# Two-layer steps of a conditioned layer pair: ScalarE's gelu halves before yt and x_hi, GpSimd's second low half before its power, VectorE's x_lo after the second statistics

## The reference, cut to what matters

```
kind 0 or 1:  out = gelu(x @ w1 + b1) @ w2 + b2            (two layers)
kind 2:       out = gelu(gelu(x @ w1 + b1) @ w2 + b2) @ w3 + b3   (three layers)
x1  = layernorm(x + out) * gamma + beta
h   = gelu(x1 @ down_W.T + down_b)
h   = h @ expert_W[domain].T + expert_b[domain] + domain_emb[domain]
out = layernorm(h @ up_W.T + up_b + x1) * ln_gamma + ln_beta
```

## Time and profile before

| | |
|---|---|
| median of 3 runs | 278.79 us (278.51 to 279.04) |
| profiled execution, own time | 277.94 us |
| its span | 276.1 us |
| TensorE matmuls | 252.9 us busy, 92% of the span |
| VectorE | 203.0 us, 74% |
| ScalarE | 191.2 us, 69% |
| GpSimd | 174.7 us, 63% |
| granted TensorE clock, mean | 0.985 |

### The profile page before, as it was taken

The page is one execution under the profiler, slowest core; times in us unless marked ns, Lnnn a source line. Parts: engine busy times, 40 slices in busy tenths (PEclk is TensorE's granted clock), DMA queues, the critical chain, the costliest instruction groups (busy, mean ns, idle before and its releaser), DMA issues.

```text
span 276.1 us, 8026 instructions
## 1 busy us (share of the span) xinstructions
PE 252.9 (92%) x2114; PEld 219.2 (79%) x2115; DVE 203.0 (74%) x715; ACT 191.2 (69%) x450; POOL 174.7 (63%) x190
## 2 busy tenths in 40 slices
PE   7998999999999988999999999999999999999850
PEld 7798889989989977878887777788888888778630
DVE  6779453294495485878888877888888888878871
ACT  3587579668768765867777777777777777777730
POOL 3134565455876876867777677677776777677480
PEclk9999999999999999999999999999999999999995
DMA  6373011101212202232323222333232323222224
GB/s 181 101 251 70 6 36 42 23 22 40 61 39 58 67 28 57 67 85 80 91 76 95 76 76 79 83 85 82 80 85 77 94 76 95 76 77 71 54 66 92
DMA packets 41640, 20.71 MB, mean 75 GB/s; under 512 B 37431, under 2 KB 39181, under 8 KB 41614
## 3 DMA queue, kind: packets, MB, share of 16 engines
q1 hardware_dynamic: 37785, 12.23, 18.5%
q0 software_dynamic: 2592, 7.08, 7.3%
q10 hardware_dynamic: 1236, 1.06, 1.5%
HBM read 11.69 MB, written 8.65 MB: 74 GB/s over the span
## 4 chain that ended last, share of the span: by engine, by line
PE 58%; ACT 13%; issue 11%; DVE 8%; POOL 5%; DMA 2%; DVEq 1%; ACTq 1%; SPq 1%; POOLq 0%
PE ps_h L1082 18%; PE ps_z L1150 12%; PE ps_t L1172 9%; PE ps_z L1155 6%; ACT yt L931 5%; ACT x_hi L883 4%; ACT h_hi L897 3%; POOL h_lo L481 2%; PE ps_z L1117 2%; PE ps_u L1202 2%; PE ps_t L1253 2%; POOL rs L488 1%; PE ps_t L1256 1%; PE ps_t L1254 1%; DMA out<-o 1%
## 5 line engine op out<-in xcount | busy, mean ns | idle before, releaser
L481 POOL TENSOR_TENSOR h_lo<-h,h_hi 128x256 fp32r<-128x256 f32 (+1 forms) x75 | 70.6, 942 | 45.3 <-ACT h L897 42.1
L488 POOL TENSOR_TENSOR rs<-ve,minus_half 128x4 f32<-128x4 f32 (+1 forms) x38 | 41.0, 1079 | 32.2 <-DVE ve L699 32.0
L904 ACT ACTIVATE zn<-ps_z,nm,rs 128x256 f32<-128x256 f32 x66 | 33.7, 562 | 31.4 <-DVE nm L703 30.9
L687 DVE BATCH_NORM_STATS2 st<-ps_z 128x6 f32<-128x256 f32 x66 | 24.9, 418 | 31.5 <-PE ps_z L1155 31.5
L897 ACT ACTIVATE h_hi<-ps_h,per_feature_sb 128x256 fp32r<-128x256 f32 x84 | 38.9, 496 | 12.3 <-PE ps_h L1082 8.2
L931 ACT ACTIVATE yt<-ps_t,per_feature_sb 128x256 f32<-128x256 f32 x66 | 34.1, 574 | 17.5 <-PE ps_t L1172 17.4
L1150 PE MATMUL ps_z<-last_hi,h_hi 128*128 (+1 forms) x132 | 35.8, 305 | 6.7 <-ACT h_hi L897 6.7
L897 ACT ACTIVATE h<-ps_h,per_feature_sb 128x256 f32<-128x256 f32 x84 | 38.8, 498 | 0.0
L661 DVE TENSOR_TENSOR x_lo<-x,x_hi 128x512 fp32r<-128x512 f32 x33 | 23.5, 712 | 19.8 <-ACT x_hi L883 19.8
L1202 PE MATMUL ps_u<-tables,stack 65*64 x132 | 35.6, 392 | 0.3 <-ACT stack L915 0.3
L1202 PE MATMUL ps_u<-second_table,stack 65*64 65x256 f32 x132 | 35.5, 392 | 0.0
(11 more groups left out here) (150 smaller groups left out, 658.3 us busy)
## 6 DMA issues: line engine op xcount, KB each, us to landing
x<-in_x_feat SPq DMA_DIRECT2D x130, 64.0 KB
out<-o SPq DMA_DIRECT2D x20, 64.0 KB, 2.0
out<-o,out_rows_now POOLq DMA_INDIRECT x54
last_sb<-in_last_w SPq DMA_DIRECT2D x1, 768.0 KB, 5.0
w_sr_sb<-in_w_sr SPq DMA_DIRECT2D x1, 512.0 KB, 4.0
w_sr_sb<-in_w_sr ACTq DMA_DIRECT2D x1, 512.0 KB, 5.0
w_two_sb<-in_w_two SPq DMA_DIRECT2D x1, 512.0 KB, 5.6
per_unit_sb<-in_per_unit SPq DMA_DIRECT2D x1, 268.1 KB
```

Of the source, the lines that this page charges most:

```text
L481: pool.tensor_tensor(dst, full, high.bitcast(F32), ALU.subtract).then_inc(ready, 1)
L488: pool.tensor_tensor(RS[p][:, norms, :], VE[p][:, norms, :], half_of_two[:, norms, :], ALU.pow).then_inc(rstd, 1)
L904: ins = act.activation(ZN[:, t, :], ZP[p][:, t, :], ACT.Identity, bias=NM[p][:, t:t + 1], scale=RS[p][:, 0, t:t + 1])
```

## The change

Three lists are reordered; no instruction is added or dropped.

ScalarE: in two-layer steps the second gelu half comes straight after the first, ahead of `yt` and `x_hi`. In the step in which the last three-layer slot is finished, `yt` stays first and both gelu halves follow. GpSimd: in the same steps the low half of the second gelu comes ahead of the power. VectorE: in every step up to the last but two, the statistics of `ps_u` come ahead of `x_lo`, and their moments behind it.

```
@@ gpsimd, step of a two-layer slot
                 with pool.Else():
                     for slot in on_slot(g, -1, where):
                         low(h2l[:, 0, :], h2[:, 0, :], h2h[:, 0, :], h0_full, h0_lo, g + 1)
-                    powers(g, i, p, where)
                     for slot in on_slot(g, -1, where):
                         low(h2l[:, 1, :], h2[:, 1, :], h2h[:, 1, :], h1_full, h1_lo, g + 1)
+                    powers(g, i, p, where)
@@ vector
                 variances(p, BOTH)
+                for slot in on_slot(g, 2, where):
+                    second_stats(slot, p)
                 for slot in on_slot(g, -2, where):
                     input_low(slot, p)
                 for slot in on_slot(g, 2, where):
+                    second_moments(slot, p, q)
                     if where == LAST2:
-                        last_variances(slot, p, q)
-                    else:
-                        second_stats(slot, p)
-                        second_moments(slot, p, q)
+                        dve.wait_ge(stat[1], 2 * TT * slot + 2 * TT)
+                        variances(q, SECOND)
@@ scalar
                         with act.If(g < b_sr):
...
                             for k in kind:
                                 first_of_two(k, True)
+                                second_of_two(k)
                         with act.Else():
                             for k in kind:
                                 first_of_two(k, False)
+                                second_of_two(k)
                             for slot in on_slot(g, 1, where):
                                 residual_norm(slot, q, where)
                     next_input(g, i, p, where)
-                    for k in kind:
-                        second_of_two(k)
```

More of the change, by code:

```diff
@@ L991, in _ @@
                         first_of_two(kind[0], False)
+                        second_of_two(kind[0])
                     else:
```

## The result

The changed kernel takes 283.27 us (median of 4 runs, 283.00 to 283.64) where the kernel before takes 278.92 in the same job (4 runs, 278.51 to 279.66). The ratio is 1.0151, with a 95% interval from 1.0128 to 1.0174: 4.35 us slower, where I had predicted 5.8 us faster. The time lies inside the range, the direction was wrong. The profiled execution took 283.44 us.

The account below looks back on a forecast made before the run. ScalarE's order was taken to set the 6.37 us two-layer step. 277.94 - 5.1 - 1.0 + 0.2 = 272.0 us profiled, 273.0 forecast for the median, range 267.5 to 284.0.

Parts of the forecast that it names:

- The step that failed: GpSimd, low half ahead of the power: cost 0 in the steady step, stores out about 1.2 us earlier.
- The mechanism of the late signals: TensorE's signals in dense steps: cause unknown; second gelu half assumed to start 0.2 us beyond 208.33.
- Second gelu ahead of `yt`: ScalarE, two-layer steps: removes the last layer's wait for `h_hi`, gaining 0.23 us a step, 5.1 us over 22 steps.
- GpSimd, the single places: Step after the three-layer ones and last two-layer step: waits for the low half go, net 0.6 and 0.4 us.
- VectorE, 0 and +0.2 us: `x_lo` behind the statistics of `ps_u`: 0 in the steady step, 0.2 us lost in all in three-layer steps.
- The slow rival: ScalarE: second gelu waits for its late signal, `yt` behind it; +0.37 us a step, 286.1 us on the median; chance 0.23.
- The fast rival: TensorE waits for nothing, its own stream bounds: steps of 5.9 us, 267.4 us on the median; chance 0.22.
- The density reading: Full internal trace-record queues can hold an engine back, so a denser step would keep its late signals; no run showed it.

Follow-up runs that it names:

- holding job: Any of the three follow-up jobs in which the kernel before, unchanged, took about 279 us.
- The undone part: Changed kernel with GpSimd's order of before, the power ahead of the second low half: 275.89 us, ratio 0.9875 to the kernel before.
- free job: Any of the three follow-up jobs in which the kernel before, unchanged, took about 266 us.
- later stores: Changed kernel with one more GpSimd subtraction (0.7 us) into a spare tile ahead of its two scattered stores: 280.36 us, ratio 1.0022 to the kernel before.

## Why the prediction was wrong, point by point

**The step that failed** is in the part on GpSimd's low half: "The stores behind go out about 1.2 us earlier; nothing waits for them", and the cost of 0 that it was given. I asked who waits for the stores and not what they hold up. In a holding job, in most steps, the instruction that waits for TensorE starts only 1.4 to 1.9 us behind the second store's start. Against the first layer the second store went out 0.57 us earlier (+0.32 instead of +0.89). At its old place the hold reached `yt` by way of the transposes' signal (whether that of `ps_h1` was held there too, nothing shows, since nothing waited for it); at the new one it reaches the first half by way of `ps_h0`, at the head of all of ScalarE's work. The undone part shows the price: 282.77 against 275.89 in one job, 6.9 us.

**The mechanism of the late signals.** I had written that I did not know what makes them late, and took a middle value, 0.2 us, for the lateness of the second half. What came was a first half 1.05 us later (+2.17 instead of +1.12). Two GpSimd rows would have shown `yt` 1.77 behind the store in this step; I had cited GpSimd's other rows and not the stores, and not the step at 116.95, where the first half was held already.

**Second gelu ahead of `yt`, -0.23 us a step.** Some pieces were right: the last layer follows the down-projection after 0.59 (0.54 said), the wait for `h_hi` is gone, and two pairs behind each other put `yt` 1.44 behind the first half (205.44 to 206.88; 4 x 0.36). With VectorE's part and without GpSimd's the gain was 3.5 us in a holding job, where the term and the +0.2 make 4.9. In total the steps went the other way. From the transposes of the first two-layer step to those of the last, 22 steps, it was 252.49 - 112.58 = 139.91 us and is 258.53 - 111.22 = 147.31: +7.40 us instead of -5.1, or +0.34 a step instead of -0.23. The two last transposes, before and after:

```profile
252.49 0.60 PE L1172 MATMUL ps_t<-ident,zn 128*128 128x128 f32 x4
```

```profile
258.53 0.60 PE L1174 MATMUL ps_t<-ident,zn 128*128 128x128 f32 x4
```

**GpSimd, the single places, -1.0 us.** These came. After the three-layer steps the last layer's wait of 0.91 us is gone and the transposes wait 0.47 for `zn`, as forecast. The down-projection of that step before, and the rows after:

```profile
107.70 0.61 PE L1215 MATMUL ps_d<-yt,per_feature_sb 128*64 128x128 f32 x8
```

```profile
107.08 0.61 PE L1217 MATMUL ps_d<-yt,per_feature_sb 128*64 128x128 f32 x8
...
108.65 0.62 PE L1157 MATMUL ps_z<-last_hi,h_lo 128*128 x4
...
111.22 0.66 PE L1174 MATMUL ps_t<-ident,zn 128*128 128x128 f32 x4 [0.47 <-ACT zn L905]
```

From the down-projection to the transposes it was 112.58 - 107.70 = 4.88 us and is 4.14: 0.74 less, where I had 0.6. In the last two-layer step the 0.42 us of the earlier trace rows is gone as well: from its transposes to the end of the span it was 276.1 - 252.49 = 23.61 us and is 281.7 - 258.53 = 23.17, 0.44 less. Together 1.18.

**VectorE, 0 and +0.2 us.** `zn` starts 0.59 ahead of the next first layer instead of 0.32, and does not wait. Undoing the part changed the time by 0.24 us (283.01 against 282.77), within the noise. The 0.2 us in three-layer steps had the wrong sign: the down-projection behind them starts 0.62 us *earlier* than before (107.08 against 107.70), and with VectorE's part undone it is back at 107.76.

**The sum.** 7.40 - 1.18 - 0.62 = 5.60 us, the difference of the two spans (281.7 - 276.1); the profiled executions differ by 5.5 (283.44 - 277.94). The forecast had -5.1 - 1.0 + 0.2 for the same three terms, so the first term missed by 12.5 us, and the other two, better than forecast, gave 1.0 back.

**The rivals.** The slow rival, 286.1 us with a chance of 0.23, came nearest, but by luck: it had the second half held and a wait of that `h_hi`. In the steady steps of the trace the second half never waits; it waits once, 0.56 us, in the step at 115.89. The fast rival, all signals early, is what happens in a free job, though from a kernel before of 266.46 us, so it is worth 2.2 us there and not 11: such a job gives that time back to the kernel before as well. Its least step of 5.9 was a little long too; without waits the mean is 5.81.

**What delays a signal.** The Trainium skill's page Perfetto Trace Analysis, section "Tensor Engine Instruction (MATMUL, LD_WEIGHTS)", says that a matmul's end is worked out from its size and the semaphore comes when PSUM has acknowledged. The holding traces agree with a signal that comes after the row's end (1.32 us). In the free trace `yt` starts 0.03 us behind the row's end, so the modelled end itself isn't far off. The density reading that I had attached to the Trainium skill's page NOTIFIC — the notification-queue block, section "Overflow: three behaviours, one of which stalls the engine", would have kept the signals late in the dense step without stores; the trace does not agree with that.

**What stays open.** What differs between a holding and a free job; no view shows it. By what way the stores reach TensorE's signals: their issue on GpSimd and the data that they move were only left out together, and only once, in two executions of a holding job. In the same stretch VectorE copies `second_table` (207.62 before, 203.88 after); no run left that out, so it may have a part in it. And why not every signal at that place is held. In the first two-layer step before, `yt` starts at 113.22, only 0.94 behind the second store, and hardly late:

```profile
112.28 1.02 POOL L514 DMA_INDIRECT out<-o,out_rows_now  x1 [0.30 <-issue]
```

So the stores are needed for the hold, as the run without them shows, but they are not enough for it. The three-layer steps tell nothing: no engine waits there for a signal that falls due just behind the second store.

## What to carry to other kernels

When a signal comes later than the row that should send it, look across *all* engines for an instruction that stands at about the same distance ahead of the late start in several steps, and treat everything that moves it as an edit to the critical path. An edit that only changes an order can move transfers past signals without adding a wait; "nothing waits for them" is not a price. Read the odd step as well as the steady one: the one at 116.95 had shown the late first half beforehand. And time a kernel in several jobs: this change is worth -0.8% in one kind and +1.3 to +1.5% in the other.

## What the runs showed of the hardware

- In some jobs TensorE's signals come late around GpSimd's scattered stores (0.9 to 1.3 us each in GpSimd's row) and come on time without them. Where a signal is held, the first instruction that waits for it starts 1.4 to 1.9 us behind the second store's start (before, after, their repeats, GpSimd's and VectorE's parts undone, later stores). For the kernel before that makes 279 us out of 266, for the changed one 283 out of 264.
- The kernel before took 265.8 to 267.5 us in every run of the three free jobs, and 277.9 to 280.0 in all but two of the holding ones and the prediction's (288.84 and 1357.94), so what decides holds for a whole job; and one chip had both kinds.
- The edge of the hold isn't sharp. By the ends of the rows, a signal of the kernel before that was due 0.04 us ahead of the second store passed (207.32 against 207.36). With GpSimd's part undone one that was due 0.06 ahead was held (166.66 against 166.72), and one that was due 0.16 behind the store passed (173.61 against 173.45).
